# Issuing the token-tile loads of the cluster pass from SyncE alone instead of SyncE and ScalarE

## The chip, the cores and the metric

The kernel runs as one program on all 8 cores of one Trainium2 chip. Cores 0 to 3 lie on one die and cores 4 to 7 on the other. No data passes between the cores. The metric is device time in microseconds of the slowest core. In what follows PE is TensorE, DVE is VectorE, ACT is ScalarE, POOL is GpSimd and SP is SyncE. Each of these has its own instruction stream, worked off strictly in order, and a load that an engine issues is an instruction of that stream, marked SPq, ACTq or POOLq in the trace.

## What is computed

One transformer block on 4 batches of 2048 tokens with 4096 features: layer norm, causal attention with 32 heads and ALiBi bias, and beside it a dense layer whose rows are masked by a soft cluster assignment. The part that the change touches is the mask (cut from the reference, where `x` is the layer-normed input of all 8192 tokens):

```python
dots = jax.nn.softmax(x @ centroids.T / TEMPERATURE, axis=-1)
hits = dots > THRESHOLD
query_sel = jnp.any(hits, axis=1)
cluster_sel = jnp.any(hits, axis=0)
row_sel = cluster_sel[assignments]
dense = x @ weight.T + bias
out = jnp.where(query_sel[:, None] & row_sel[None, :], dense, 0)
```

`cluster_sel` needs the 64 dot products of every one of the 8192 tokens, so each core goes over the whole transposed input `xT_all` (4096 by 8192, f32) by itself.

## The kernel before

The kernel has five stages, one after the other. Stage 1 normalises the tokens. Stage 2 computes K and V for all tokens of the batch. Stage 3, which the change touches, lies between about 2500 and 4300 us. Stage 4 is attention, and stage 5 the output projection with the masked dense layer.

Stage 3 alternates two generators, 16 times each, and every engine gets the instructions of the two in that order:

- `p2b_gen`, one round for 256 columns of the query projection. It goes over 32 chunks of 128 features. For chunk `kc` it loads a weight tile `qw` (128 KB), casts it to bf16 (`qb`), and does four matmuls into `qp`. There are six buffers. Even buffers are loaded by SP and cast by DVE; odd ones are loaded by ACT and cast by ACT. At the end of the round ACT evicts four tiles (`qo`).
- `p3_gen`, one round for a group `tg` of 512 tokens. It goes over 32 chunks `kc`. Chunk number `tg*32+kc` modulo 6 gives the buffer `s`. A tile `d3x` of 128 by 512 f32 (256 KB) is loaded; DVE casts it to bf16 (`d3b`); ACT (even `s`) or POOL (odd `s`) squares it into `d3q`; and PE does three matmuls into `d3pd`: centroids by `d3b`, a column of ones by `d3b`, a column of ones by `d3q`. After the 32 chunks comes a closing part: a chain of small operations on `d3r`, `d3w`, `d3t`, `d3e`, `d3g` between DVE, ACT and PE, which turns the sums into softmax hits.

The order on the engines is the program's. In a `p3_gen` round before the change SP issues the loads of buffers 0, 1 and 2, on the semaphores `dsq`, and ACT those of buffers 3, 4 and 5, on the semaphores `acq`. Each load waits until the cast (`b_done3[s]`) and the square (`q_done3[s]`) that last read its buffer are done. On ACT the stream of six chunks is: square 0; square 2; load 3; load 4; square 4; load 5. `DV`, `AC` and `PO` also wait for their own last operation before each new one. Engine `SY` (SP) computes nothing. The two lines that choose the issuing engine are 520 and 521 (`xqe, xch = ...`); the load itself is line 522. All DMA starts appear in the trace under line 99, computing operations under line 80, and matmuls under line 87, which are lines of helpers, so that tile names tell them apart.

Of the kernel before, what the change touches and what calls it, by code (L numbers as in the profile page):

```python
# [106 lines left out]
def build_program():  # L107
# [29 lines left out]
    with es:  # L137
# [28 lines left out]
        AC = Eng(es, nc, nc.scalar, "ac", auto=True)  # L166
        PO = Eng(es, nc, nc.gpsimd, "po", auto=True)
        SY = Eng(es, nc, nc.sync, "sy", auto=False)

        sq = [Ch(es, nc, f"sq{i}") for i in range(10)]  # L170
# [5 lines left out]
        acq = [Ch(es, nc, f"acq{i}") for i in range(3)]  # L176
# [16 lines left out]
        def emit_all():  # L193
# [36 lines left out]
            with contextlib.ExitStack() as e1:  # L230
# [19 lines left out]
                for t in range(24):  # L250
                    own = t >= 16
                    s = t % 2
# [80 lines left out]
                for fp_ in range(NH):  # L333
                    col0 = DM + fp_ * 256
                    ins = None
                    for kc in range(NKC):
                        s = (fp_ * NKC + kc) % NSL
# [49 lines left out]
            with contextlib.ExitStack() as e2:  # L387
# [8 lines left out]
                with contextlib.ExitStack() as e23:  # L396
# [110 lines left out]
                    def p3_gen():  # L507
# [6 lines left out]
                        for tg in range(16):  # L514
                            ps_d = ps_d2[tg % 2]
                            ins = None
                            for kc in range(NKC):
                                s = (tg * NKC + kc) % 6
                                sqe = AC if s % 2 == 0 else PO
                                xqe, xch = ((SY, dsq[s]) if s < 3  # L520
                                            else (AC, acq[s - 3]))
                                xqe.dma(xch, xtt[s][:],
                                        xT_all[kc * 128:(kc + 1) * 128,
                                               tg * 512:(tg + 1) * 512],
                                        waits=[(DV.ch, b_done3[s]),
                                               q_done3[s]])
                                b_done3[s] = DV.op(
                                    "tensor_copy", xbb[s][:], xtt[s][:],
                                    waits=[(xch, xch.n),
                                           (PE.ch, x_done[s])])  # L530
                                if sqe is AC:
                                    q_done3[s] = (AC.ch, AC.op(
                                        "activation", xsq[s][:], xtt[s][:],
                                        AF.Square,
                                        waits=[(xch, xch.n),
                                               (PE.ch, x_done[s])]))
                                else:
                                    q_done3[s] = (PO.ch, PO.op(
                                        "tensor_tensor", xsq[s][:], xtt[s][:],
                                        xtt[s][:], ALU.mult,  # L540
                                        waits=[(xch, xch.n),
                                               (PE.ch, x_done[s])]))
                                PE.raw("matmul", ps_d[0:64, :],
                                       cv[:, kc, 0:64], xbb[s][:],
                                       start=(kc == 0), stop=(kc == NKC - 1),
                                       waits=([(DV.ch, b_done3[s]),
                                               q_done3[s],
                                               (AC.ch, psd_free_ac[tg % 2]),
                                               (DV.ch, psd_free_dv[tg % 2])]
                                              if kc == 0 else  # L550
                                              [(DV.ch, b_done3[s]),
                                               q_done3[s]]))
                                PE.raw("matmul", ps_d[64:65, :], onescol[:],
                                       xbb[s][:],
                                       start=(kc == 0), stop=(kc == NKC - 1),
                                       tile_position=(0, 64),
                                       skip_group_check=True)
                                ins = PE.raw("matmul", ps_d[96:97, :],
                                             onescol[:], xsq[s][:],
                                             start=(kc == 0),  # L560
                                             stop=(kc == NKC - 1),
                                             tile_position=(0, 96),
                                             skip_group_check=True)
                                x_done[s] = PE.mark(ins)
# [73 lines left out]

                    g2 = p2b_gen()
                    g3 = p3_gen()  # L640
                    done = object()
                    for i in range(16):
# [66 lines left out]
                with contextlib.ExitStack() as e4:  # L709
# [71 lines left out]
                    for h in range(NH):  # L781
                        s = h % 2
# [188 lines left out]
                with contextlib.ExitStack() as e5:  # L971
# [48 lines left out]
                    for fp_ in range(NKC // 2):  # L1020
                        for kc in range(NKC):
                            s = (fp_ * NKC + kc) % NSL
# [188 lines left out]
```

How the kernel before makes its waits and increments, by code:

```python
    def inc(self, instr, k=1):  # L52
        instr.then_inc(self.h, k)
        self.n += k
        return self.n
# [9 lines left out]
    def wait(self, ch, val):  # L65
        if val <= 0:
            return
        key = id(ch)
        if self._waited.get(key, -1) >= val:
            return
        assert val <= ch.n, f"wait {val} > produced {ch.n}"
        self.e.wait_ge(ch.h, val)
        self._waited[key] = val
# [119 lines left out]
        def emit_all():  # L193
# [903 lines left out]
                                    ALU.add, waits=[(xq, xq.n)])  # L1097
                                t_free[tp] = ev_dv = DV.op(
                                    "tensor_tensor", osb[so][:], t1[tp][:],
                                    t3[:],
                                    ALU.add, waits=[(gq[4 + so], o_done[so])])
                                PO.dma(gq[4 + so],
                                       outT[fc * 128:(fc + 1) * 128,
                                            rc * 512:(rc + 1) * 512],
                                       osb[so][:], waits=[(DV.ch, DV.ch.n)])
                                o_done[so] = gq[4 + so].n
                    PO.e.wait_ge(gq[4].h, gq[4].n)
                    PO.e.wait_ge(gq[5].h, gq[5].n)
```

## Time and profile before

| what | us |
|---|---|
| median of two timed runs | 6985.7 (6947.74 and 7023.67) |
| the profiled execution | 6680.78 |
| its span on the slowest core (core 1) | 6679.2 |
| spans of the eight cores | 6643.8 to 6679.2 |
| PE busy with matmuls | 4509.5 (68%) |
| DVE busy | 1833.2 (27%) |
| ACT busy | 1448.6 (22%) |
| POOL busy | 669.8 (10%) |

The profiled execution is 305 us shorter than the median of the timed ones. All durations below are of the profiled execution, core 1. Busy shares are means over all five stages; the stage at hand has to be read from its own stretch. In the page's list of DMA issues, the loads of `d3x` appear as 257 from SP with a median of 3.7 us from issue to landing, and 255 from ACT with a median of 3.0 us; the weight loads `qw` as 256 from each, with 2.4 and 2.2 us.

### The profile page before, as it was taken

How to read it: one execution, taken by the hardware profiler on the slowest of the kernel's cores; microseconds unless marked ns; L12 is line 12 of the kernel's file. 1: busy time of each engine (PE TensorE's matmuls, PEld its weight loads, DVE VectorE, ACT ScalarE, POOL GpSimd, SP SyncE). 2: the span in 40 equal slices, each digit the busy share in tenths (PEclk: the TensorE clock that was granted, in tenths of full speed). 3: DMA queues.
4: the chain of work that ended last, by engine and by line, in shares of the span. 5: the costliest groups of instructions: out<-in, count | busy, mean ns of one | idle time of the engine just before them, and what ended most of it. 6: DMA issues, size and time to landing. Idle time of an engine off the chain costs nothing.

```text
span 6679.2 us, 80075 instructions; the slowest of 8 cores (6643.8 to 6679.2 us)
## 1 busy us (share of the span) xinstructions
PE 4509.5 (68%) x20715; PEld 1925.2 (29%) x20715; DVE 1833.2 (27%) x4169; ACT 1448.6 (22%) x2628; POOL 669.8 (10%) x1061
## 2 busy tenths in 40 slices
PE   2229999999999976555555555445555548877887
PEld 1114444444434431111111111122232323333333
DVE  4431111111111112323232324355533322222222
ACT  4420000000000002222222222133344432222222
POOL 0021111111111101212121212100000000000000
PEclk9999999999999987777777777666655559988998
DMA  4432222222222233333333333221111124444444
GB/s 127 134 109 81 89 86 79 92 87 81 88 87 85 83 120 119 118 119 118 119 118 116 121 114 122 91 92 44 48 48 48 45 87 145 146 137 148 148 141 136
DMA packets 518299, 687.07 MB, mean 103 GB/s; under 512 B 60129, under 2 KB 390881, under 8 KB 517857
## 3 DMA queue, kind: packets, MB, share of 16 engines
q1 hardware_dynamic: 266866, 346.56, 16.4%
q10 hardware_dynamic: 227952, 259.89, 12.8%
q0 software_dynamic: 23040, 75.52, 3.3%
q8 instruction: 183, 3.00, 0.2%
q14 instruction: 258, 2.11, 0.1%
HBM read 606.22 MB, written 75.50 MB: 102 GB/s over the span
## 4 chain that ended last, share of the span: by engine, by line
PE 45%; DMA 22%; DVE 14%; ACT 9%; issue 7%; ACTq 1%; SPq 1%; DVEq 1%; POOL 1%; POOLq 0%
PE p2p L87 27%; DMA qw<-w_attn 8%; DMA d3x<-xT_all 6%; PE f5b L87 5%; PE f5a L87 5%; ACT a4e L80 5%; DMA f5f<-ffn_wT 4%; DVE statc L80 2%; PE d3pd L87 2%; PE a4po L87 2%; DVE d3r L80 2%; PE a4pt L87 1%; DVE a4o L80 1%; DVE d3b L80 1%; ACT p1n L80 1%
## 5 line engine op out<-in xcount | busy, mean ns | idle before, releaser
L87 PE MATMUL p2p<-xn_fm,p2b 128*128 128x512 bf16 x8192 | 1834.9, 387 | 147.9 <-DVE p2b L80 141.3
L87 PEld LDWEIGHTS p2p<-xn_fm,p2b 128*128 128x128 bf16 x8192 | 809.5, 99 | 1173.1 <-issue 247.8
L87 PE MATMUL qp<-xno,qb 128*128 128x512 bf16 x2048 | 517.3, 402 | 306.3 <-DVE qb L80 172.9
L87 PE MATMUL f5a<-ofm,f5pb 128*128 128x512 bf16 x2048 | 543.7, 389 | 232.2 <-DVE f5pb L80 217.5
L87 PE MATMUL f5b<-xno,f5fb 128*128 128x512 bf16 x2048 | 538.9, 386 | 24.3 <-DVE f5fb L80 23.6
L87 PE MATMUL a4po<-a4a,a4e 128*128 128x129 bf16 x2304 | 329.4, 268 | 293.9 <-ACT a4e L80 280.3
L80 DVE CAST p2b<-p2w 128x256 bf16<-128x256 f32 x512 | 152.4, 298 | 1343.7 <-PE p2p L87 1250.7
L80 DVE CAST d3b<-d3x 128x512 bf16<-128x512 f32 x512 | 361.1, 705 | 538.3 <-DMA d3x<-xT_all 475.4
L80 ACT ACTIVATE p2o<-p2p,battn 128x512 bf16<-128x512 f32 x128 | 88.2, 689 | 1908.3 <-PE p2p L87 1898.8
L87 PE MATMUL d3pd<-d3b,centbf 128*64 128x512 bf16 x512 | 271.8, 531 | 335.0 <-POOL d3q L80 229.1
L80 ACT ACTIVATE a4e<-a4t 128x128 bf16<-128x128 f32 (+3 forms) x616 | 258.2, 419 | 600.3 <-DVE a4t L80 539.3
L87 PEld LDWEIGHTS qp<-xno,qb 128*128 128x128 bf16 x2048 | 194.6, 102 | 624.0 <-issue 455.8
L87 PE MATMUL p1t<-identbf,p1n 128*128 128x128 bf16 x768 | 105.2, 302 | 365.8 <-ACT p1n L80 285.3
L87 PEld LDWEIGHTS f5a<-ofm,f5pb 128*128 128x128 bf16 x2048 | 202.8, 100 | 489.0 <-issue 260.1
L87 PEld LDWEIGHTS a4po<-a4a,a4e 128*128 128x128 bf16 x2304 | 187.9, 113 | 525.9 <-issue 520.2
L80 POOL CAST p2b<-p2w 128x256 bf16<-128x256 f32 x512 | 205.4, 401 | 1315.5 <-PE p2p L87 1179.7
L80 POOL TENSOR_TENSOR d3q<-d3x 128x512 bf16<-128x512 f32 x256 | 294.7, 1151 | 402.8 <-DMA d3x<-xT_all 352.6
L87 PE MATMUL a4ps<-a4q,a4k 128*128 128x512 bf16 (+3 forms) x768 | 326.2, 459 | 0.1
L87 PEld LDWEIGHTS f5b<-xno,f5fb 128*128 128x128 bf16 x2048 | 198.6, 99 | 293.2 <-issue 78.8
L80 DVE CAST f5fb<-f5f 128x256 bf16<-128x256 f32 x256 | 75.3, 294 | 724.7 <-DMA f5f<-ffn_wT 578.4
L80 ACT ACTIVATE d3q<-d3x 128x512 bf16<-128x512 f32 x256 | 161.6, 631 | 483.7 <-DMA d3x<-xT_all 348.6
L87 PE MATMUL d3pd<-d3q,onescol 128*1 128x512 bf16 x512 | 252.6, 493 | 0.0
(109 smaller groups left out, 3162.5 us busy)
## 6 DMA issues: line engine op xcount, KB each, us to landing
d3x<-xT_all SPq DMA_DIRECT2D x257, 256.0 KB, 3.7
p2w<-w_attn ACTq DMA_DIRECT2D x512, 128.0 KB, 2.1
p2w<-w_attn SPq DMA_DIRECT2D x512, 128.0 KB, 2.1
f5f<-ffn_wT ACTq DMA_DIRECT2D x512, 128.0 KB, 2.7
f5p<-w_proj SPq DMA_DIRECT2D x512, 128.0 KB, 2.9
d3x<-xT_all ACTq DMA_DIRECT2D x255, 256.0 KB, 3.0
qw<-w_attn SPq DMA_DIRECT2D x256, 128.0 KB, 2.4
qw<-w_attn ACTq DMA_DIRECT2D x256, 128.0 KB, 2.2
```

The source lines that it names most:

```text
L80: instr = getattr(self.e, method)(*args, **kw)
L87: return getattr(self.e, method)(*args, **kw)
```

## The change

The loads of buffers 3, 4 and 5 are issued by SP as well. They signal the semaphores `sq[7]`, `sq[8]` and `sq[0]` in place of `acq[0]` to `acq[2]`. Their waits on `b_done3[s]` and `q_done3[s]`, the tiles, the sizes and the order of chunks stay. Nothing else is touched.

```diff
                                 xqe, xch = ((SY, dsq[s]) if s < 3
-                                            else (AC, acq[s - 3]))
+                                            else (SY, [sq[7], sq[8],
+                                                       sq[0]][s - 3]))
                                 xqe.dma(xch, xtt[s][:],
                                         xT_all[kc * 128:(kc + 1) * 128,
                                                tg * 512:(tg + 1) * 512],
```

`sq[0]` served four small loads at the start of the kernel; `sq[7]` and `sq[8]` were unused. The kernel's barriers wait for all of `sq` that has been used.

## Rows read from the trace of the kernel before

**Rows 1.** Stretches: from:to, length, busy PE, PEld, DVE, ACT, POOL, granted clock, DMA share, GB/s.

```profile
2546.62:4273.17 1726.55, 972.57 (x3591) 298.31 (x3591) 580.49 (x1073) 386.54 (x739) 312.63 (x288) 0.75 0.38 119
3442.57:3488.73 46.16, 28.04 (x96) 6.43 (x96) 22.33 (x33) 10.10 (x17) 18.78 (x17) 0.67 0.57 186
3488.73:3509.65 20.92, 1.48 (x9) 0.88 (x10) 10.22 (x23) 5.65 (x12) 0.00 (x0) 0.53 0.02 7
3509.65:3550.92 41.27, 32.02 (x128) 12.04 (x128) 5.66 (x18) 6.49 (x16) 0.00 (x0) 0.95 0.36 109
```

**Rows 2.** Chain that ended last, stretch 2546 to 4273, shares by line.

```profile
by line: DMA qw<-w_attn 28.9%; DMA d3x<-xT_all 24.5%; PE d3pd L87 7.5%; issue 6.9%; DVE d3r L80 5.7%; DVE d3b L80 5.3%; PE qp L87 4.5%; POOL d3q L80 2.4%; ACT qo L80 2.4%; ACT L80 2.2%; ACT d3e L80 1.3%; ACTq L72 1.1%; ACT qb L80 1.0%; DVE 
```

**Rows 3.** Timeline of ACT inside a round: start, us, operation [idle before, what ended it].

```profile
3456.72 0.82 ACTq L99 DMA_DIRECT2D d3x<-xT_all  x2
3461.56 0.63 ACT L80 ACTIVATE d3q<-d3x 128x512 bf16<-128x512 f32 x1 [4.34 <-DMA d3x<-xT_all]
3461.69 0.33 ACTq L99 DMA_DIRECT2D d3x<-xT_all  x1
3463.13 0.82 ACTq L99 DMA_DIRECT2D d3x<-xT_all  x2
3466.69 0.63 ACT L80 ACTIVATE d3q<-d3x 128x512 bf16<-128x512 f32 x1 [3.05 <-DMA d3x<-xT_all]
```

**Rows 4.** Tile d3x, whole kernel: duration ns min/median/max; then landing times.

```profile
L80 DVE CAST d3b<-d3x x512: 426/428/1294, 2538.7 to 4269.9; 128x512 bf16<-128x512 f32 x171
L80 ACT ACTIVATE d3q<-d3x x256: 630/631/633, 2549.7 to 4265.9; 128x512 bf16<-128x512 f32 x128
L80 POOL TENSOR_TENSOR d3q<-d3x x256: 1034/1040/1299, 2550.8 to 4269.7; 128x512 bf16<-128x512 f32 x128
L99 ACTq DMA_DIRECT2D d3x<-xT_all x255: 334/334/649, 2550.5 to 4265.3; - x128
DMA to landing us min/median/max: 2.5/3.4/6.5
```

**Rows 5.** Timeline: evictions and first closing operation, first and last of 16 rounds.

```profile
2546.62 3.03 ACT L80 ACTIVATE qo<-qp,bq 128x512 bf16<-128x512 f32 x4 [1.32 <-PE qp L87]
2596.16 0.69 DVE L80 TENSOR_SCALAR d3r<-d3pd 1x512 f32<-1x512 f32 x1 [2.16 <-PE d3pd L87]
...
4223.80 3.03 ACT L80 ACTIVATE qo<-qp,bq 128x512 bf16<-128x512 f32 x4 [1.38 <-PE qp L87]
4273.17 0.69 DVE L80 TENSOR_SCALAR d3r<-d3pd 1x512 f32<-1x512 f32 x1 [2.16 <-PE d3pd L87]
```

**Rows 6.** Timeline of PE: first matmul of four chunks, at either clock.

```profile
3453.67 0.64 PE L87 MATMUL d3pd<-d3b,centbf 128*64 128x512 bf16 x1
...
3454.76 0.64 PE L87 MATMUL d3pd<-d3b,centbf 128*64 128x512 bf16 x1
...
3457.20 0.40 PE L87 MATMUL d3pd<-d3b,centbf 128*64 128x512 bf16 x1
...
3457.84 0.40 PE L87 MATMUL d3pd<-d3b,centbf 128*64 128x512 bf16 x1
```

**Rows 7.** Timeline: DVE and POOL with their inputs landed, side by side.

```profile
3337.87 5.03 DVE L80 CAST d3b<-d3x 128x512 bf16<-128x512 f32 x6 [3.42 <-DMA d3x<-xT_all]
3337.97 3.59 POOL L80 TENSOR_TENSOR d3q<-d3x 128x512 bf16<-128x512 f32 x3 [5.05 <-DMA d3x<-xT_all]
```

**Rows 8.** Loads of xno, 32 of 256 KB issued by SP alone: stretches; landing times.

```profile
2483.00:2490.00 7.00, 0.00 (x0) 0.00 (x0) 0.00 (x0) 0.00 (x0) 0.00 (x0) 0.50 1.01 350
2490.00:2500.00 10.00, 0.00 (x0) 0.00 (x0) 0.00 (x0) 0.00 (x0) 0.00 (x0) 0.50 1.05 389
...
DMA to landing us min/median/max: 2.9/6.9/9.7
```

**Rows 9.** Chain near the end of a projection round: start, us, what.

```profile
3419.49 2.17 DMA qw<-w_attn
...
3421.86 4.80 DMA qw<-w_attn
...
3426.86 3.20 DMA qw<-w_attn
```

## The prediction

> **What bounds the kernel now.** I read the page's 40 slices first, to find where `d3x` is used (about 2500 to 4300 us), then the stretches, the chain of waits, and the timeline of one round. The stage takes 1727 us, and no engine fills it: PE is busy 973 us of it and the DMA engines 38% of their time [rows 1]. The reader should see three parts in a round. The chunk loop of the cluster pass is 46 us long in the round shown, its closing part with the start of the next projection 21 us, the rest of the projection 41 us [rows 1]. Over the 16 rounds the time from the start of the four evictions to the first closing operation is 47.2 to 53.8 us; the first round has 49.5 and the last 49.4, and the mean of the 16 is 50.0 [rows 5]. Less 3.0 us of evictions that leaves **47.0 us for 32 chunks**, 1.47 us each.
>
> In the chain, waiting for `d3x` loads takes 24.5% of the stage, about 423 us, or 26 us a round; `qw` loads take 28.9% [rows 2]. So the loop waits for transfers although the DMA engines move only 186 GB/s there at a share of 0.57, and although six buffers exist [rows 1]. ACT's timeline says why [rows 3]. ACT issues loads 3 and 4, and its next instruction is the square of buffer 4, which has to wait for the load just issued: ACT stands 4.34 us, and 3.05 us the next time. Only then comes load 5, and only after two more squares the next loads 3 and 4. Buffers 3 to 5 are thus never loaded ahead; each waits out a whole landing time on the stream that should have fetched the next. In the rows, load 5 starts 0.13 us after the square that was held up. DVE, in order, waits for these buffers too, and SP's own loads wait for DVE and the squares.
>
> **The change, part by part.**
>
> *Removed from ACT:* 255 issues of 334 ns [rows 4], five or six a round, and above all their position. ACT keeps 16 squares of 0.63 us a round, 10.1 us; it no longer bounds anything.
>
> *Added to SP:* as many issues. With 32 a round at about 0.33 us SP is occupied 11 us of a loop of 30. SP now goes over the buffers in order; load i+6 is issued when cast and square of chunk i are done. Queued behind SP's last `d3x` load are the weight loads of the next projection. They wait until chunk 25 is consumed, which is some 6 us before the loop ends, and the closing part of 15 to 21 us follows before they are needed; that costs nothing, and it would cost something only if these loads slipped by more than that part. The three changed semaphores add waits at the barriers only, on transfers long landed: nothing.
>
> *New pace of the loop.* Four limits can follow ACT's stall. PE needs 1.09 us a chunk at 1.2 GHz and 0.64 us at 2.4 GHz, from the starts of successive chunks [rows 6]; the granted clock of the loop is 0.67 now [rows 1], between the levels, with the rise coming only after PE has worked on end. DVE and POOL, with all inputs there, took 5.03 us for six casts and three squares, 0.84 us a chunk [rows 7]; alone a cast is 0.43 and a POOL square 1.04, and both stretch to 1.29 when side by side [rows 4]. The DMA engines moved 186 GB/s at a share of 0.57 [rows 1], which is 326 GB/s at a full share, or 0.80 us for 262 KB; `xno` loads from SP's queue alone reached 350 to 389 GB/s [rows 8]. The round trip of a buffer is a landing of 3.4 us (6.5 at most), up to 1.3 us of cast and square, and 0.3 us of issue: 5.0 us over six buffers is 0.83 us, with the 6.5 us landing 1.35 us [rows 4]. Three of the four lie between 0.8 and 0.85. They do not hit each other perfectly, and PE starts at the low clock (in the round shown it rose only between 3454.8 and 3457.2 us [rows 6]; I estimate the first nine chunks), so I take **0.95 us** (0.84 and 1.09 are the ends).
>
> The exclusion of DVE and POOL is the one place where a rule bears on this pace. The Trainium skill, page "SBUF — State Buffer", states that the two lock a shared port pair for a whole instruction and the loser blocks fully. By that rule six casts and three squares would take 5.7 us, or 0.95 us a chunk; the row has 5.03 us, so the trace agrees that they hinder each other, though by less.
>
> *New length of the loop.* When the evictions end, all six buffers are loaded and cast (now only three are), and POOL's three squares are done. ACT's first square takes 0.6 us and frees buffer 0; the load of chunk 6 lands some 4 us later, say at 4.5. From there 26 chunks at 0.95 are 24.7 us, and the last square and matmuls 1.8 us: **31.0 us**. PE is not later: nine chunks at 1.09 and 23 at 0.64 are 24.5 us. Gain 47.0 − 31.0 = 16.0 us a round. The ends: 0.6 + 3.4 + 26 × 0.84 + 1.8 = 27.6 us (gain 19.4), and PE at the low clock throughout, 0.8 + 32 × 1.09 = 35.7 us (gain 11.3).
>
> *Given back in the projection.* SP runs ahead, so the first loads of a round are issued near the end of the projection, on whose path ACT's own `qw` loads lie. With three such loads the two `qw` loads beside them took 4.80 and 3.20 us instead of 2.17 each, 3.7 us lost [rows 9]. Now it is six. The added 786 KB take 2.4 us at 326 GB/s; doubling the loss would be 3.7 us. I take **2.7 us** a round, with 0 (hidden behind matmuls that are still outstanding there) and 3.7 as ends.
>
> *Sum:* 16 × (16.0 − 2.7) = 213 us. The profiled execution would go from 6680.8 to **6468 us** (−3.2%). Ends: 16 × 19.4 = 310 us off, and 16 × (11.3 − 3.7) = 122 us off.
>
> **The timed runs.** They have 6948 and 7024 us, median 6985.7, 305 us above the profiled execution; nothing in the profile says where these lie. I take the saving over unchanged: 6985.7 − 213 = **6773 us**. Should the changed kernel's runs be as quick as the profiled execution, they would show 6468. The range has to hold both.
>
> **Rivals.**
> 1. *The loop stays at the low clock or waits on landings* (chance 0.15). For it: three matmuls of a chunk with small gaps may not count as steady work, and the clock was 0.67 with the present gaps [rows 1]. Against it: the projection runs at 0.95 with PE busy 32 of 41 us [rows 1], and 23 chunks at 0.64 with a pace of 0.95 give a similar share. Price: 122 us off, 6559 in the profile, 6864 timed. 2% is 134 us here, and this falls just within.
> 2. *Only issue time is saved* (0.10). If buffers 3 to 5 were late because of the transfers themselves, moving their issue would bring only ACT's 255 × 0.334 = 85 us at most: 6596, or 6901 timed, −1.3%. The rule behind this is in the Trainium skill, page "DMA: Bandwidth & Descriptors", section "Issuing engines are not separate DMA queues": all issuing engines feed the same 16 DMA engines, and spreading the issue only saves sequencer time, which is usually small. Against the rival stands the DMA share of 0.57 in the loop and a 4.34 us stall right behind an issue on the same stream [rows 1, 3]: the order of the stream costs more than the issue.
> 3. *One queue slows the landings: slower* (0.07). With six loads outstanding on one queue beside seven other cores, landings may lengthen. The `xno` loads, deeper queued, had a median of 6.9 and a maximum of 9.7 us [rows 8]. Break-even is a loop of 47.0 − 2.7 = 44.3 us, so (44.3 − 6.9) / 26 = 1.44 us a chunk, a round trip of 8.6 us or a landing of 7.0 us. At 9.7 us the trip is 11.3 us, 1.88 a chunk, the loop 55.8 us, and the round 11.5 us longer: 184 us more, 6865 in the profile, 7170 timed. Against it: SP's queue alone carried 389 GB/s [rows 8], and the present maximum of a `d3x` landing is 6.5 us.
>
> **How the numbers follow.** My forecast has 0.68. A change of about 2% is what a measurement can tell from none. Faster by over 2%: nearly all of the forecast and a little of rival 1, 0.70. Within 2%: the rest of rival 1, rival 2 and the middle of rival 3's span, 0.24. Slower: 0.06. The likeliest case's own range is 6675 to 6865 us on the timed median. The stated range runs from 6465 (the forecast on the profiled execution's level) to 6895 (rival 2's level on the timed one). It is wide because of the 305 us between the levels, not because of the change.
>
> **What would show it.** In the changed profile ACT's idle time before its squares should fall from 3 to 4 us to under 1 in the loop, and `d3x` in the stage's chain from 24.5% to under 12%; the loop should be 28 to 36 us, its DMA rate above 240 GB/s, the clock above 0.75, landings of `d3x` longer than now (4 to 5 us median), the two or three last `qw` loads of a projection longer. Stages 1, 2, 4 and 5 keep their times. I am wrong if landings reach 7 us, if the loop stays over 40 us, or if the projection grows by more than 4 us a round.

## The result, and the profile after

| | before | after |
|---|---|---|
| median of the timed runs, us | 6933.17 (10 runs, 6670.59 to 7138.81) | 6788.93 (11 runs, 6462.27 to 6993.06) |
| ratio | 1 | 0.9683, 95% interval 0.9664 to 0.9702 |
| profiled execution, us | 6680.78 | 6473.06 |
| span of the slowest core, us | 6679.2 | 6471.5 |
| granted clock, mean of that core | 0.831 | 0.848 |

In many timed runs the cores of a die had a lower granted clock for a time, which makes the medians of both kernels longer and scattered; the ratio, and every ratio below, is taken from executions or dies where that wasn't so (before about 6675 us, after about 6462 us). A ratio of 0.9683 is 212 us off 6681; the two profiled executions differ by 207.7 us. The change makes the kernel **3.2% faster**.

The gain comes from the stage that the change touches: it is 223 us shorter between the two slowest cores, and 211 us on core 5 alone (1714 before). First the stretches of the changed kernel's slowest core, core 5, with the columns of [rows 1]: the stage from the first evictions to the last closing operation, the chunk loop of one round, and the time from its end to the next evictions (closing part and projection).

```profile
2550.85:4054.18 1503.33, 908.22 (x3591) 298.07 (x3591) 557.20 (x1070) 385.48 (x739) 310.13 (x288) 0.82 0.44 136
3144.21:3174.98 30.77, 23.78 (x96) 6.18 (x96) 19.12 (x27) 10.07 (x16) 18.74 (x17) 0.89 0.80 253
3174.98:3237.27 62.29, 33.31 (x137) 12.85 (x137) 17.16 (x43) 12.11 (x28) 0.00 (x0) 0.84 0.29 87
```

The stage was 1727 us and is 1503. The loop shown is 30.8 us where it was 46.2, at 253 GB/s instead of 186 and at a clock of 0.89 instead of 0.67 [rows 1]. As in [rows 5], a loop is read from the end of the evictions to the first closing operation:

```profile
3141.18 3.03 ACT L80 ACTIVATE qo<-qp,bq 128x512 bf16<-128x512 f32 x4 [1.38 <-PE qp L87]
...
3174.98 0.68 DVE L80 TENSOR_SCALAR d3r<-d3pd 1x512 f32<-1x512 f32 x1 [1.12 <-PE d3pd L87]
...
3237.27 3.03 ACT L80 ACTIVATE qo<-qp,bq 128x512 bf16<-128x512 f32 x4 [1.38 <-PE qp L87]
```

Over the 16 rounds of a core, and then over the eight cores, this gives:

| us a round | loop | rest (closing part and projection) |
|---|---|---|
| before, core 1 | 47.0 | 61.7 |
| after, core 5 | 32.0 | 62.9 |
| before, eight cores (46.5 to 48.0; 59.6 to 61.7) | 47.2 | 60.5 |
| after, eight cores (30.7 to 32.0; 61.5 to 63.9) | 31.4 | 62.7 |

So 15.8 us a round are won in the loop and 2.2 given back outside it: 13.6 × 16 = 218 us, against 208 to 212 measured for the whole kernel.

The chain of waits over the stage in the changed kernel:

```profile
by line: DMA qw<-w_attn 34.4%; DMA d3x<-xT_all 14.0%; issue 8.3%; DVE d3b L80 7.7%; DVE d3r L80 6.6%; PE qp L87 5.4%; PE d3pd L87 4.8%; POOL d3q L80 3.9%; ACT qo L80 3.0%; ACT L80 2.5%; ACT d3e L80 1.5%; ACTq L72 1.0%; ACT qb L80 0.9%; DVEq
```

`d3x` falls from 24.5% of 1727 us, 423 us, to 14.0% of 1503 us, 210 us [rows 2]. Beside it DVE's casts `d3b` grow from 5.3% (92 us) to 7.7% (116 us) and POOL's squares from 2.4% (41 us) to 3.9% (59 us), so in part the loop now waits for work instead of transfers. The largest item is `qw`, 517 us where it was 499; it is the subject of a later experiment.

The timeline of ACT in the changed loop (start, us, operation, idle before it and what ended it), which answers to [rows 3]:

```profile
3144.30 2.07 ACT L80 ACTIVATE d3q<-d3x 128x512 bf16<-128x512 f32 x3
3148.63 0.63 ACT L80 ACTIVATE d3q<-d3x 128x512 bf16<-128x512 f32 x1 [2.25 <-DMA d3x<-xT_all]
3151.05 0.63 ACT L80 ACTIVATE d3q<-d3x 128x512 bf16<-128x512 f32 x1 [1.80 <-PE d3pd L87]
3153.26 0.63 ACT L80 ACTIVATE d3q<-d3x 128x512 bf16<-128x512 f32 x1 [1.57 <-PE d3pd L87]
3154.28 0.63 ACT L80 ACTIVATE d3q<-d3x 128x512 bf16<-128x512 f32 x1 [0.40 <-DMA d3x<-xT_all]
```

ACT starts the round with three squares in a row, since all six buffers are loaded, and 6 of its 13 later waits in this loop are for PE to free a `d3q` buffer: that is the other end of the pipeline. The stalls of 3.05 and 4.34 us behind an issue of its own are gone, and no wait in this loop is over 2.25 us. The landings themselves are no shorter:

```profile
DMA to landing us min/median/max: 2.8/4.1/7.0
```

They were 3.4 us in the median [rows 4]. Each transfer takes longer and the loop is faster, because more of them are on their way at once. An estimate of their mean number is the loads issued within a loop times the median landing, over the length of the loop: 29 × 3.4 / 47.2 = 2.1 before and 26 × 4.1 / 31.4 = 3.4 after.

### The profile page after: what moved, and what is told of

Same layout as the page of the kernel before. It is cut to its first block, busy times and chain, and to the rows that moved or that the text cites. A ratio compares the mean times of both kernels' runs of the same rounds, so it can differ in the third digit from the quotient of the medians.

```text
span 6471.5 us, 80168 instructions; the slowest of 8 cores (6429.3 to 6471.5 us)
## 1 busy us (share of the span) xinstructions
PE 4450.8 (69%) x20715; PEld 1929.1 (30%) x20715; DVE 1811.4 (28%) x4169; ACT 1444.8 (22%) x2628; POOL 667.6 (10%) x1061
## 4 chain that ended last, share of the span: by engine, by line
PE 47%; DMA 19%; DVE 14%; ACT 9%; issue 7%; POOL 1%; SPq 1%; DVEq 1%; ACTq 1%; POOLq 0%
PE p2p L87 28%; DMA qw<-w_attn 8%; PE f5b L87 6%; PE f5a L87 6%; ACT a4e L80 5%; DMA d3x<-xT_all 3%; DMA f5f<-ffn_wT 3%; DVE statc L80 2%; DVE d3b L80 2%; PE a4po L87 2%; DVE d3r L80 2%; PE a4pt L87 1%; PE qp L87 1%; DVE a4o L80 1%; ACT p1n L80 1%
## 5 line engine op out<-in xcount | busy, mean ns | idle before, releaser
L80 DVE CAST d3b<-d3x 128x512 bf16<-128x512 f32 x512 | 339.1, 662 | 330.8 <-DMA d3x<-xT_all 231.5
L87 PE MATMUL d3pd<-d3b,centbf 128*64 128x512 bf16 x512 | 228.7, 447 | 170.1 <-ACT d3q L80 69.8
L80 POOL TENSOR_TENSOR d3q<-d3x 128x512 bf16<-128x512 f32 x256 | 292.2, 1141 | 178.7 <-DMA d3x<-xT_all 111.6
L80 ACT CAST f5fb<-f5f 128x256 bf16<-128x256 f32 x256 | 103.6, 405 | 674.1 <-DMA f5f<-ffn_wT 553.5
L80 ACT CAST qb<-qw 128x256 bf16<-128x256 f32 x256 | 103.5, 404 | 605.3 <-DMA qw<-w_attn 558.8
```

Source lines behind the costliest of these rows:

```text
L80: instr = getattr(self.e, method)(*args, **kw)
L87: return getattr(self.e, method)(*args, **kw)
```

## The experiments

The theory to be tested: the cost before was not the transfers, nor ACT's time to issue them, but that ACT issued a load too shortly before its data was used. Its rivals: what counts is how many loads an engine issues, or which queue carries them.

### ACT issues its loads earlier

```diff
+                            for k in range(AHEAD):      # AHEAD = 4
+                                load(k)
                             for kc in range(NKC):
-                                xqe.dma(xch, xtt[s][:], ...)
+                                if kc + AHEAD < NKC:
+                                    load(kc + AHEAD)
```

The diff is shortened. `load(k)` is the old load with the old choice of engine (SP for `s < 3`, ACT otherwise). SP's stream holds nothing but loads in the same order as before, so what moves is the place of ACT's loads among its squares.

> ACT keeps issuing the loads of buffers 3, 4 and 5, on its own queue, but in every round each load (SP's and ACT's) is issued four chunks before its chunk is consumed; the tiles, sizes and number of loads per queue are those of the kernel before. Theory of position (what cost was that ACT waited on a load that it had only just issued): the loop falls from 47.0 us to 33 to 38 us a round. It doesn't quite reach the 32.0 us of the changed kernel, because ACT's first loads of a round can only be issued after the four evictions and land 3 to 4 us into the loop. Ratio to the kernel before 0.970 to 0.982. Rival of queue or issue (what helped was that ACT issues fewer DMAs, or that SP's queue is better): nothing is moved off ACT here, so the loop stays at 44 to 47 us, ratio 0.99 to 1.00.

6485.3, 6489.1 and 6509.0 us, against about 6675 us of the kernel before: ratio 0.971. The loop is 33.8 us on core 5 and 34.8 on core 1; the rest is 61.8 and 60.7 us. ACT in one round:

```profile
3136.89 0.82 ACTq L100 DMA_DIRECT2D d3x<-xT_all  x2
3137.86 0.63 ACT L81 ACTIVATE d3q<-d3x 128x512 bf16<-128x512 f32 x1 [0.36 <-ACT qo L81]
3137.93 0.33 ACTq L100 DMA_DIRECT2D d3x<-xT_all  x1
3138.58 0.63 ACT L81 ACTIVATE d3q<-d3x 128x512 bf16<-128x512 f32 x1
3142.18 0.63 ACT L81 ACTIVATE d3q<-d3x 128x512 bf16<-128x512 f32 x1 [2.97 <-DMA d3x<-xT_all]
```

ACT still issues its share of the loads, all of them on its own queue, and nearly the whole gain is there. Its first loads of a round (here at 3136.89) can't be issued before the evictions are nearly over, so a wait of 2.97 us stays exposed at the start. That fits the 3.1 us by which the loop, 34.5 us over eight cores, is longer than in the changed kernel; no run separates it. What the change did through SP is in the main a matter of when, not of which queue.

### The two sets of buffers exchanged

```diff
-                                xqe, xch = ((SY, dsq[s]) if s < 3
-                                            else (AC, acq[s - 3]))
+                                xqe, xch = ((AC, acq[s]) if s < 3
+                                            else (SY, dsq[s - 3]))
```

> The kernel before with the two sets of buffers exchanged: ACT issues the loads of buffers 0, 1 and 2, SP those of 3, 4 and 5. Each queue has as many loads and bytes as in the kernel before. ACT's stream becomes load 0, square 0, load 1, load 2, square 2, square 4, so two of its squares stand right behind their own load instead of one. Theory of position: two exposed landings of 3.4 us per six chunks on ACT, the loop 50 to 56 us, ratio 1.007 to 1.03. Rival of queue or issue: the counts are the same, loop 47 us, ratio 0.998 to 1.002.

6761 to 6772 us: ratio 1.014. The loop is 52.8 us on core 0 and 52.4 on core 1, 5.4 us longer than before, with the same loads on each queue. ACT's timeline shows two stalls in six chunks where [rows 3] has one:

```profile
3114.85 0.82 ACTq L99 DMA_DIRECT2D d3x<-xT_all  x2
3119.76 1.35 ACT L80 ACTIVATE d3q<-d3x 128x512 bf16<-128x512 f32 x2 [4.36 <-DMA d3x<-xT_all]
3120.56 0.34 ACTq L99 DMA_DIRECT2D d3x<-xT_all  x1
3123.53 0.63 ACT L80 ACTIVATE d3q<-d3x 128x512 bf16<-128x512 f32 x1 [2.41 <-DMA d3x<-xT_all]
```

The count of loads and bytes per queue is ruled out as the cause: it is unchanged here but for two loads, and the time is not. The edit also turns ACT's two squares `s = 0` and `s = 2` into squares that stand right behind their own load, where the kernel before had one, `s = 4`.

### Only the load of buffer 4 moved

```diff
                                 xqe, xch = ((SY, dsq[s]) if s < 3
+                                            else (SY, sq[8]) if s == 4
                                             else (AC, acq[s - 3]))
```

> The kernel before with only the load of buffer 4 moved from ACT to SP; ACT keeps the loads of buffers 3 and 5. ACT's stream becomes square 0, square 2, load 3, square 4, load 5, so no square stands behind its own load. A third of the issues is moved. Theory of position: most of the gain comes with this one load, loop 33 to 38 us, ratio 0.970 to 0.982. Rival of issue count: a third of the 15 us of the whole change, loop 42 us, ratio 0.989 to 0.991.

6582 to 6609 us, ratio 0.988. The loop is 40.5 us on core 5 and 41.6 on core 1: 6 of the 15 us, not most of them. My expectation missed, and the number falls on the rival's. The timeline says why: loads 3 (here at 3090.97) and 5 (at 3092.29) are still issued just before their use. DVE waits 2.66 us for buffer 3, as it did for such buffers before the change, and ACT still has waits of up to 3.66 us in this loop.

```profile
3089.00 0.63 ACT L80 ACTIVATE d3q<-d3x 128x512 bf16<-128x512 f32 x1 [3.66 <-DMA d3x<-xT_all]
3090.84 0.63 ACT L80 ACTIVATE d3q<-d3x 128x512 bf16<-128x512 f32 x1 [1.21 <-DMA d3x<-xT_all]
3090.97 0.33 ACTq L99 DMA_DIRECT2D d3x<-xT_all  x1
...
3092.29 0.34 ACTq L99 DMA_DIRECT2D d3x<-xT_all  x1
3094.22 0.63 ACT L80 ACTIVATE d3q<-d3x 128x512 bf16<-128x512 f32 x1 [1.42 <-DMA d3x<-xT_all]
3094.73 1.60 DVE L80 CAST d3b<-d3x 128x512 bf16<-128x512 f32 x2 [2.66 <-DMA d3x<-xT_all]
```

Load 3 stands behind square 2, so it can't be issued before chunk 2 is being consumed, and chunk 3 is next. My picture in the prediction, a stall because the square directly follows its own load, was too narrow. A rival count of issues gives this run's 6 us, but it can't give the first experiment's 12 to 13 us with no issue moved. What fits both is the *lead*: how many chunks lie between a load and the last square ahead of it on the issuing engine. For loads 3, 4 and 5 that is 1, 2 and 1 chunks in the kernel before, and 5, 6 and 5 in the first experiment. The lead alone doesn't explain the exchange of the buffers: there it is 2, 1 and 2 chunks for loads 0, 1 and 2, no less than before, and the loop is 5.4 us longer. What differs there is how often the issuing engine itself has to wait for a load that it has just issued: twice in six chunks, not once.

### A lead of two chunks

The first experiment with `AHEAD = 2`.

> The kernel before with every load issued two chunks before its chunk is consumed, each queue keeping its loads (the run with four chunks had loops of 33.8 to 34.8 us, the kernel before has 47.0 with none, and moving buffer 4's load alone gave 41, where loads 3 and 5 had a lead of about one chunk). Theory of lead (the cost is the landing time less the lead, wherever the load stands): two chunks of about 1.1 us hide 2.2 of 3.7 us of landing, loop 36 to 40 us. Rival of adjacency (only a load directly ahead of its own square costs): as good as four chunks, 33 to 35 us.

The loop is 36.4 to 37.5 us over the eight cores, mean 37.1. Only the loops of this one execution, 6784 us, are read. Its excess lies outside the touched stage: cores 2 to 5 enter the stage at 2751 to 2812 us and the others at 2526 to 2546, and the last stage takes 1310 to 1316 us on those others where it takes 1167 to 1178 on cores 2 to 5. Outside the loops of the stage core 7 was granted a clock of 0.81, and the changed kernel's core 5 one of 0.79.

With `AHEAD` at 0 the loop was 47 us, at 2 it is 37, at 4 it was 34. Behind which square the loads stand gives leads of 1 to 2, 3 to 4, and 5 to 6 chunks for the three. No square stands right behind its own load in the last two, so a theory in which only the neighbour counts would give them the same time; it gave 33 to 35 us for this run. The theory of lead gave 36 to 40. How the exposed part of a landing falls with the lead isn't measured beyond these three points.

### Three loads of the first six given back to ACT

```diff
                                 xqe, xch = ((SY, dsq[s]) if s < 3
                                             else (SY, [sq[7], sq[8],
+                                                       sq[0]][s - 3])
+                                            if kc >= 6
+                                            else (AC, [sq[7], sq[8],
                                                        sq[0]][s - 3]))
```

> The changed kernel, but the loads of buffers 3, 4 and 5 among the first six chunks of each round are issued by ACT as in the kernel before; from the seventh chunk SP issues all. Only three loads of a round can then be issued during the projection. If the burst of six loads is what lengthened the time between the closing part and the next evictions (61.7 to 62.9 us on the slowest cores, 59.7 to 63.9 us over the cores looked at), that time falls back by 1 to 2 us a round, while the loop starts with late buffers and grows from 32.0 to 35 to 38 us. If the burst costs nothing, that time stays as in the changed kernel and only the loop grows.

6502.95 us in the profiled execution, 30 us above that of the changed kernel. The rest of a round is 61.2, 60.2, 60.6 and 61.5 us on cores 0, 1, 2 and 5, mean 60.9 against 62.7 in the changed kernel and 60.5 in the one before; the loop is 35.8 to 36.2 us. So the 1.8 to 2.2 us a round outside the loop are the price of the longer burst. In the chain of the changed kernel it is seen on the `qw` loads beside it, which take 4.36, 2.93 and 2.98 us instead of 2.1:

```profile
3217.37 2.13 DMA qw<-w_attn
...
3219.70 4.36 DMA qw<-w_attn
...
3224.27 2.93 DMA qw<-w_attn
...
3227.68 2.98 DMA qw<-w_attn
...
3230.87 2.15 DMA qw<-w_attn
```

Before, two of them were long [rows 9], and in this run, on core 5, one is, with its neighbours at 2.2 us and less:

```profile
3234.32 2.19 DMA qw<-w_attn
...
3236.71 4.15 DMA qw<-w_attn
```

The price is worth paying: the three early loads that cost 1.8 us save 4.6 us of loop.

### POOL's squares given to ACT

```diff
-                                sqe = AC if s % 2 == 0 else PO
+                                sqe = AC
```

on top of the change.

> The changed kernel with POOL's 16 squares a round given to ACT, which then has 32 of 0.63 us. DVE's casts are alone on what they shared with POOL, so 0.43 us each. If DVE and POOL side by side set the new pace of the loop (0.84 us a chunk), the loop falls from 32.0 to 27 to 29 us, ratio to the kernel before 0.953 to 0.960. If the landings set it (DMA share 0.80 in the changed loop), the loop stays at 31 to 33 us, ratio 0.965 to 0.972.

6407 to 6431 us, ratio 0.961, a hair above the expected 0.960. The loop is 28.2 us on core 0 and 27.4 on core 1, mean 27.8 over eight cores, where the changed kernel has 31.4. DVE's casts by tile, duration minimum, median and maximum:

```profile
L80 DVE CAST d3b<-d3x x512: 426/427/429, 2530.1 to 3962.2; 128x512 bf16<-128x512 f32 x171
```

No cast is longer than 429 ns, where the maximum was 1294 before [rows 4] and 1291 in the changed kernel. So the squares on POOL did hold the changed loop back by 3 to 4 us a round. Two things went with them, and the run doesn't separate the two: casts that stretch beside POOL, and POOL's own squares of 1.04 us and more in place of ACT's 0.63. In the changed kernel's chain of the stage the casts hold 116 us and POOL's squares 59, and PE's idle time before the matmuls of `d3pd` was 68 us for POOL's squares and 32 us for the casts. The Trainium skill, page "SBUF — State Buffer", section "Who interferes with whom", explains such stretching by a port pair that the two lock for a whole instruction. The casts' maximum of 1.29 us, a cast of 0.43 plus most of a POOL square of 1.04, agrees with that; the 5.03 us of [rows 7], where whole instructions one after the other would take 5.7, agrees in direction only.

What limits the loop that is left isn't shown. In a loop of this run the DMA share is 0.81 at 267 GB/s, hardly above the changed kernel's 0.80, and PE is busy 24.6 of 29.1 us:

```profile
2999.90:3029.00 29.10, 24.58 (x96) 6.24 (x96) 11.09 (x26) 20.15 (x32) 0.54 (x1) 0.83 0.81 267
```

### The same cure for the projection's weights

```diff
-                                qeng, qch = ((SY, wsq[s]) if s % 2 == 0
-                                             else (AC, aq2[s]))
+                                qeng, qch = ((SY, wsq[s]) if s % 2 == 0
+                                             else (SY, wsq[s]))
```

on top of the change. ACT loaded and cast the odd tiles, each load just ahead of its cast.

> The changed kernel with the odd weight loads qw of the projection moved from ACT to SP as well, where they stand behind the same kind of stall: ACT issues a load and next has to cast it. Theory of lead: the projection becomes PE-bound, 128 matmuls of 0.22 us and a start at the low clock, 30 to 33 us in place of 41 to 43; the time outside the loop falls from 62.9 to 50 to 54 us, the loop stays at 31 to 33 us. Ratio to the kernel before 0.938 to 0.950. Rival (weights bound by transfers or PE already): time outside the loop 60 us or more, ratio 0.962 to 0.970.

6261 to 6276 us, ratio 0.940. The rest of a round is 51.1 us on core 5 and 51.2 on core 4, 11.6 us less than the changed kernel's 62.7, and the loop stays at 31.5 and 31.3. PE's matmuls of the projection, busy, mean ns, then idle before and its releasers, in the changed kernel and in this run:

```profile
L87 PE MATMUL qp<-xno,qb 128*128 128x512 bf16 x2048 | 527.5, 409 | 314.8 <-DVE qb L80 172.3 <-ACT qb L80 142.1
```

```profile
L87 PE MATMUL qp<-xno,qb 128*128 128x512 bf16 x2048 | 481.4, 400 | 171.2 <-DVE qb L80 171.2
```

The 142 us of waits for ACT's casts are gone, and the 172 us that remain are the one wait per round in which PE stands during the closing part. In the chain of the stage `qw` is no longer among the entries shown, and the matmuls of the projection take its place at the top:

```profile
by line: PE qp L87 34.3%; DMA d3x<-xT_all 13.3%; DVE d3b L80 9.1%; DVE d3r L80 8.0%; issue 7.8%; PE d3pd L87 6.1%; POOL d3q L80 4.2%; ACT qo L80 3.2%; ACT L80 3.0%; ACT d3e L80 2.0%; DVE d3g L80 1.3%; DVE ormax L80 1.1%; DVEq L72 1.1%; ACT 
```

### All of it together

```diff
-                            AC.dma(aq2[s], wft[s][:],
+                            SY.dma(aq2[s], wft[s][:],
                                    ffn_wT[...],
```

with the edits of the last two experiments, on top of the change.

> The changed kernel with three further edits: the qw loads and the stage-5 loads f5f on SP instead of ACT, and POOL's squares on ACT. If the parts add up: 176 us for qw, 40 us for the squares (as measured alone: undisturbed dies 6411 against 6471), and in the last stage, where PE is busy 952 of 1249 us and the chain holds 267 us of f5f loads, 20 to 80 us, since its rounds also wait for evictions that the edit doesn't touch. Ratio to the kernel before 0.915 to 0.940. If SP, now with all loads, becomes a bound in the last stage (64 issues of 0.33 us a round of 78 us, behind waits for residual loads), that stage grows instead and the ratio is above 0.945.

6192.0 and 6194.3 us: ratio 0.927, the fastest kernel of the study, 4.3% below the changed one. The loop is 28.3 us and the rest 50.8. The last stage, from its first `f5a` matmul to the end, takes 1180 us in the run before this one and 1141 us here:

```profile
5082.10:6262.40 1180.30, 933.34 (x4096) 401.66 (x4096) 282.96 (x703) 301.13 (x640) 34.60 (x64) 0.90 0.46 142
```

```profile
5051.80:6192.80 1141.00, 920.83 (x4096) 407.59 (x4096) 283.06 (x703) 301.11 (x640) 34.59 (x64) 0.90 0.48 147
```

That is 39 us from `f5f` alone, less than the chain's 267 us that I had named beside it: PE was busy through most of those waits. Its idle time before the `f5b` matmuls, 25.6 us, is gone; the much larger one before `f5a`, one wait at the start of each of the 16 rounds, is untouched (232 us before, 234 here). SP doesn't become a bound.

## Why the prediction was right, point by point

*What bounded the loop.* Right in substance, too narrow in its mechanism. The loop waited for transfers that were issued late, while the DMA engines had room; the first experiment shows it with nothing moved off ACT. But I tied it to the square behind its own load. Buffer 4 alone should then have brought most of the gain, and it brought 6 of 15 us. The lead of the loads counts as well as the neighbour; for buffers 3 to 5 together the two pictures give the same forecast, which is why the sum didn't suffer.

*The pace.* Predicted 0.95 us a chunk for 26 chunks, between ends of 0.84 and 1.09. By the same form of sum, with its 4.5 and 1.8 us outside the 26 chunks, (32.0 − 6.3) / 26 = 0.99 us on core 5, and (31.4 − 6.3) / 26 = 0.97 over eight cores. The term was well placed. The reason given for it, several limits of 0.8 to 0.85 us that get in each other's way, is borne out in part: taking the squares off POOL took 3 to 4 us off the loop. Which limit is left then wasn't tested.

*The clock.* Predicted above 0.75, measured 0.89 in the loop shown, where it was 0.67; over core 5's 16 loops the mean is 0.86. This was the weakest step. I had no row for the clock at such a pattern of gaps and leaned on the projection's 0.95 at a similar busy share. PE is busy 23.8 of 30.8 us in the loop shown, and the clock held. Rival 1, the low clock throughout (loop 36 us), is out.

*The landings.* Predicted 4 to 5 us, measured 4.1, maximum 7.0. Rival 3 needed 7.0 us in the mean for break-even (its sums use 6.9 us outside the 26 chunks where the forecast has 6.3, which moves its price by 10 us and no conclusion). The first experiment's loads, spread over both queues, also have a median of 4.1 us on either, so the single queue costs nothing that shows.

*Given back outside the loop.* Predicted 2.7 us a round, measured 2.2 over eight cores and 1.2 between the two slowest; returning three loads to ACT took 1.8 of it away. Right cause, slightly too high: the long `qw` loads near the end of the projection are there as forecast, and with three loads given back there is again less of them.

*Only issue time.* Rival 2 allowed 85 us; 212 came. Nor was it issue time: the first experiment moved no issue off ACT and has a ratio of 0.971. The rule named there from the Trainium skill, page "DMA: Bandwidth & Descriptors", section "Issuing engines are not separate DMA queues", that issuing from several engines saves only the sequencer's time, isn't contradicted as far as it speaks of the transfers: the rate at a full share works out at 326 GB/s before and at 253 / 0.80 = 316 after. It says nothing of what else stands in that sequencer's stream, and there the time was.

*Details that missed.* The chain's share of `d3x` was to fall under 12% and is 14.0%; ACT's idle times were to fall under 1 us and are 0.4 to 2.3 us in the loop shown: those for PE's buffers, 1.0 to 1.9 us, I hadn't counted, and those for loads still reach 2.25. The upper end of the stated range, 6895, is called rival 2's level, which is 6901 by its own sum.

*The level.* The sum, 213 us, met the 208 to 212 us of the comparison, with a loop gain of 15.8 (predicted 16.0) less 2.2 (predicted 2.7). The forecast of 6773 us against a median of 6789 owes something to chance: the medians of both kernels lie over 250 us above their profiled executions and scatter by hundreds of us.

## What to carry to other kernels

A load should be issued several chunks ahead of its use, and an engine that also consumes the tiles can only do that if the program puts the issue that far ahead in its stream; count the lead of each load in chunks, compare it with the landing time, and distrust any load that stands behind a consumer of the chunk just before it, or right ahead of a consumer on the same engine. An engine with nothing else to do, such as SP, gives that lead without a change of order, limited only by the number of buffers; the price here was some 2 us a round, because its early loads slow those of the part before. When a transfer shows in the chain while the DMA share is near a half, look at the issuing engine's timeline before touching sizes or queues, and look for the same pattern in the other loops: here it was worth 212 us in one, 194 in the next and 39 in a third.

## What the runs showed of the hardware beyond what was expected

The granted clock rose with the supply: the same 96 matmuls of a loop took 28.0 us of PE's time at a clock of 0.67 before and 23.8 us at 0.89 after, so part of the gain from removing a stall comes as faster matmuls. The clock went the other way in the exchange of the buffers, where the loops had more waits: 0.65 in the mean of core 1's loops, against 0.67 before. The 0.7 us of higher landing time (3.4 to 4.1 in the median) went with a rate of 253 instead of 186 GB/s.
